# First attention layer: the last 64 rows of two projections share the array, and every engine's order of work is written anew

## The chip, the cores and the metric

The kernel runs on one core of one Trainium2 chip. The metric is the time of one execution on the device in microseconds (us), as the median of several. Abbreviations: PE is the matmul engine TensorE, DVE is VectorE, ACT is ScalarE, POOL is GpSimd, SP is SyncE, which here only starts DMAs. DMAs move data between the device memory and the on-chip memory SBUF; matmuls write to the accumulator memory PSUM, which has banks.

## The reference, cut to what matters

The program is a model of two layers on 64 sequences of 128 tokens with 256 features. Each layer is a cross attention followed by a feed forward part. Only the first attention and the routing of the first feed forward part are touched here:

```python
q = (x @ Wq).reshape(B, N, HEADS, hd)           # x: 256 features, normalized, 16 heads of 16
k = (context @ Wk).reshape(B, M, HEADS, hd)     # context: 192 features
v = (context @ Wv).reshape(B, M, HEADS, hd)
scores = einsum('bhid,bhjd->bhij', q, k) * scale    # then the mask
attn = softmax(scores)
out = einsum('bhij,bhjd->bhid', attn, v)
x = x + out @ Wo
...
logits = layernorm(x) @ w_switch + b_switch     # 8 experts
probs = softmax(logits);  routes = probs.argmax(-1)
pos = (cumsum(one_hot(routes), axis=0) * one_hot(routes)).sum(-1) - 1
keep = pos < capacity                           # row goes to slot routes*capacity+pos
```

The context has 192 features, so a contraction over it is one full step of 128 rows and one half step of 64 rows.

## The kernel before, in words

The function phase_first_layer takes two sequences at a time, a "job"; there are 32 jobs, numbered 0 to 31. A job consists of pieces with short names, and four tables of text say in which order each engine takes them. A table entry such as `K:2` in a cyclic table (FIRST_PE_ORDER and its siblings) means that in turn k of the cycle piece K of job k-2 is done. A HEAD table gives the first pieces by job number, a TAIL table the last ones, counted back from the end (`O:1` is job 31); `headed` and `ended` put them around the cycle. The order is fixed when the program is built; on the chip each engine works through its list, and waits at semaphores for its inputs.

The pieces on PE:

- Tx transposes the normalized rows, Q, K and V are the projections (four matmuls each, 128x256 per matmul; a trace counts each float32 matmul twice, so it shows x8).
- S0 and S1 are the two rounds of scores of a job. One round fills all four PSUM banks of scores: four matmuls bring the mask in (L702), then 16 matmuls with 32 rows each (L711). Bank r may only be refilled when ACT has made the exponentials of the round before from it.
- T0.0, T0.1, T1.0, T1.1 transpose the normalized probabilities (L721), A multiplies them with the values (L732, outputs of 32 partitions each), O is the output projection.
- Tn transposes the normalized new rows, L multiplies them with the routing weights (output of 8 columns), r.n counts tokens per expert.
- F0 to F5 and B0 to B5 multiply weights for a later phase; they only need loaded weights.

Products other than scores go to four PSUM banks in turn. A piece waits until what lay in its bank four products earlier has been copied out.

On DVE, `S0.x2` is the row maximum of bank 2 of round S0, `S0.i2` the reciprocal of its row sums, a name with ^ (`K^`, `A^`, `Tn^`) copies that product out of PSUM, st and st1 are statistics of rows, mk makes mask rows. The routing has three pieces there: r.sh, r.oh and r.n^. They exist once per group of jobs, for jobs 3, 7, 11, 15, 19, 23, 27, 29 and 31. I call a turn of the cycle in which they occur a routed turn, the others plain ones. r.oh is a chain of about sixteen small dependent operations (L617 to L626), r.n^ one of six (L632 to L639). On ACT, `S0.e2` are the four exponentials of bank 2, `T0^2` a copy of a transposed bank, nm the normalization of rows. On POOL, `S0.n2` divides a bank's probabilities by their sums, rs, rs1 and nm1 normalize, put sends rows to their experts' slots (two indirect DMAs).

On SP, load(j) fetches the rows x and the context of job j. The context has two buffers; a load of job j waits until K and V of job j-2 are done. The rows have four buffers, and load(j) waits for nm1 of job j-4. The layout in memory (function lay_out, unchanged) repeats the last 64 context rows in both halves of a second 128-row block, and fills the missing 64 rows of the key weights with zeros below, those of the value weights with zeros above. K and V thus each do a second full 128-row step in which half of the rows are zeros.

The second layer, which the change does not touch, already has the paired form for its own f.K and f.V (L1653, L1662, L1664, L1665).

Of the kernel before, what the change touches and what calls it, by code (L numbers as in the profile page):

```python
# [146 lines left out]
S1.x3:0 S1.x0:0 S1.x2:0 Tx^:2 S1.i1:0 V^:0 K^:1 st:3 mk:4 K^:2 S0.x2:1 S1.i0:0 S0.x3:1 S0.x1:1 S0.i1:0 S0.x0:1
V^:1 S1.i3:0 S1.x3:1 S1.x2:1 S1.x1:1 S0.i1:1 S1.x0:1 S1.i2:0 Q^:2 S0.i0:1 S1.i0:1 S0.x0:2 S1.i1:1 S1.i2:1
S0.x2:2 S0.i3:1 S0.i2:1 A^:0 S0.x3:2 S0.x1:2 V^:2 S1.i3:1 O^:0 st1:0 S0.i3:2 S0.i1:2 S1.x2:2 S1.x3:2 S1.x1:2
Tx^:3 S1.x0:2 K^:3 Q^:3 st:4 S0.x1:3 S0.x2:3 S1.i2:2 S0.x0:3 S0.i0:2 S1.i1:2 S1.i3:2 S1.i0:2 A^:1 S0.x3:3  # L150
S0.i1:3 S0.i2:2 S0.i0:3 V^:3 O^:1 st1:1 S1.x0:3 S1.x1:3 Tx^:4 S1.x3:3 K^:4 S1.x2:3 Q^:4 S0.i3:3 st:5 S1.i1:3
# [1646 lines left out]
```

## Time and profile before

| | us |
|---|---|
| median of 3 runs (4029.2 to 4032.24) | 4030.45 |
| the profiled execution's own time | 4034.15 |
| its span, first to last instruction | 4032.1 |
| start to score round S1 of job 5 | 106.05 |
| from there to S1 of job 28 (23 turns) | 408.48 |
| from there to S1 of job 31 (mask at 568.00) | 53.47 |
| from there to the first matmul of the experts' phase (629.24) | 61.24 |
| busy over the whole span: PE / ACT / DVE / POOL | 3956.1 / 2656.5 / 2384.4 / 1852.6 |

Only the first 629 us belong to the changed phase. In a timeline, a row gives the start, the duration, engine, line, operation, output<-inputs, shapes and how many instructions were merged; in square brackets stands how long the engine was idle before it and whom it waited for. A matmul's recorded duration is longer than its share of PE, since matmuls overlap; the time that a piece takes is therefore read as the difference of two starts. A windows row gives, for each engine, the busy time and the number of instructions in that stretch, then the granted PE clock (1.00 is the full 2.4 GHz), the DMA share and GB/s. The granted clock is 1.00 in all of the middle part.

### The profile page before, as it was taken

The page shows a single profiled execution, that of the slowest core. Times are in us where ns is not written, and L with a number is a line of the kernel's source. Part 1 is how long each engine was busy: PE and PEld are TensorE (multiplying, and loading weights), DVE is VectorE, ACT ScalarE, POOL GpSimd, SP SyncE. Part 2 cuts the span into 40 slices and gives each one's busy share as a digit, 9 for nine tenths or more (in the row PEclk, how much of TensorE's full clock was granted, in tenths as well). Part 3 has the DMA queues.
Part 4 walks back from the last instruction along what each step waited for, and adds up shares of the span by engine and source line. Part 5 has one row for each costly group of instructions (what it writes and reads, how often), then busy time and mean ns, then how long its engine had stood idle before and what let it go on. Part 6 is the DMA issues. An engine that isn't in the chain of part 4 may idle for free.

```text
span 4032.1 us, 100880 instructions
## 1 busy us (share of the span) xinstructions
PE 3956.1 (98%) x38276; PEld 3369.6 (84%) x38276; DVE 2384.4 (59%) x6216; ACT 2656.5 (66%) x11851; POOL 1852.6 (46%) x1979
## 2 busy tenths in 40 slices
PE   8999999999999999999999999999999999999998
PEld 6888876667888888888888888888888888888887
DVE  6888871125566566566656656666556656666554
ACT  8998971124666666666666666666666666666765
POOL 5787872113434444444444444444444444444434
PEclk9999998999999999999999999999999999999999
DMA  3232214520000000000000000000000000000000
GB/s 103 74 106 76 67 58 147 166 81 25 15 12 15 17 14 14 14 14 14 14 13 13 14 13 21 12 12 12 13 12 12 12 12 12 13 13 12 4 4 9
DMA packets 117868, 129.74 MB, mean 32 GB/s; under 512 B 12007, under 2 KB 110677, under 8 KB 117265
## 3 DMA queue, kind: packets, MB, share of 16 engines
q1 hardware_dynamic: 105648, 109.80, 8.5%
q0 software_dynamic: 6144, 8.43, 0.7%
q8 instruction: 311, 5.10, 0.5%
q10 hardware_dynamic: 5600, 5.07, 0.4%
q14 instruction: 165, 1.34, 0.1%
HBM read 89.68 MB, written 41.94 MB: 33 GB/s over the span
## 4 chain that ended last, share of the span: by engine, by line
PE 76%; DVE 1%; ACT 1%; POOL 0%; issue 0%; DMA 0%; POOLq 0%; DVEq 0%
PE c_product L1552 35%; PE c_product L1563 14%; PE c_product L1614 11%; PE c_scores L1604 7%; PE c_product L1637 5%; PE c_product L1625 2%; PE c_product L1653 1%; PE c_product L1664 1%; DVE c_qT L1407 1%; PE c_product L1540 1%; PE c_product L1662 1%; ACT c_front_probs L1364 0%; ACT c_probs L1364 0%; PE c_product L1691 0%; DVE c_neg_max L1416 0%
## 5 line engine op out<-in xcount | busy, mean ns | idle before, releaser
L1318 POOL TENSOR_TENSOR c_probs<-c_probs,c_row_inv 128x512 f32<-128x512 f32 x744 | 766.5, 1042 | 1436.6 <-DVE c_row_inv L1419 1432.9
L1364 ACT ACTIVATE c_probs<-c_scores,c_neg_max 128x128 f32<-128x128 f32 x2976 | 1054.9, 398 | 432.7 <-DVE c_neg_max L1416 432.4
L1552 PE MATMUL c_product<-c_nodes,cell_w 128*128 128x256 f32 x4352 | 1049.7, 382 | 1.5 <-DVE c_nodes L1478 0.8
L1552 PEld LDWEIGHTS c_product<-c_nodes,cell_w 128*128 128x128 f32 x4352 | 794.8, 190 | 108.8 <-issue 7.3
L1416 DVE TENSOR_REDUCE c_neg_max<-c_scores 128x4 f32<-128x512 f32 x1024 | 664.7, 676 | 104.9 <-PE c_scores L1604 98.9
L1364 ACT ACTIVATION_READ_ACCUMULATOR c_probs<-c_scores,c_neg_max 128x1 f32 x2976 | 703.5, 236 | 0.0
L1370 ACT COPY c_probsT<-c_product 128x512 f32<-128x512 f32 x744 | 416.6, 616 | 235.9 <-PE c_product L1614 229.4
L1364 ACT ACTIVATE c_front_probs<-c_scores,c_neg_max 128x128 f32<-128x128 f32 x1120 | 404.6, 406 | 176.6 <-DVE c_neg_max L1416 176.4
L1563 PE MATMUL c_product<-cell_w,c_nodes 128*128 128x256 f32 x1792 | 435.3, 383 | 0.5 <-DVE c_x L1469 0.5
L474 ACT ACTIVATE a_probs<-a_scores,a_neg_max 128x128 f32<-128x128 f32 x1024 | 360.4, 410 | 47.9 <-DVE a_neg_max L545 47.6
L1614 PE MATMUL c_product<-consts_sb,c_probs 128*128 128x128 f32 x2976 | 385.8, 273 | 0.1
L1318 POOL TENSOR_TENSOR c_front_probs<-c_front_probs,c_row_inv 128x512 f32<-128x512 f32 x280 | 287.1, 1041 | 202.7 <-DVE c_row_inv L1419 202.0
L1614 PEld LDWEIGHTS c_product<-consts_sb,c_probs 128*128 128x128 f32 x2976 | 347.4, 141 | 37.6 <-POOL c_probs L1318 0.9
L1563 PEld LDWEIGHTS c_product<-cell_w,c_nodes 128*128 128x128 f32 x1792 | 330.3, 190 | 56.5 <-issue 15.4
L1407 DVE TENSOR_SCALAR c_qT<-c_product,cell_b 128x256 f32<-128x256 f32 x372 | 162.7, 478 | 288.7 <-PE c_product L1552 288.5
L1552 PE MATMUL c_product<-c_oT,cell_w 128*128 128x256 f32 x1240 | 318.4, 379 | 0.1
L427 POOL TENSOR_TENSOR a_probs<-a_probs,a_row_inv 128x512 f32<-128x512 f32 x256 | 264.9, 1056 | 80.7 <-DVE a_row_inv L548 80.6
L1419 DVE RECIPROCAL c_row_inv<-c_row_sum 128x4 f32<-128x4 f32 x1024 | 168.5, 169 | 222.6 <-ACT c_probs L1364 195.1
L1407 DVE TENSOR_SCALAR c_kT<-c_product,cell_b 128x256 f32<-128x256 f32 x372 | 162.7, 478 | 227.4 <-PE c_product L1552 227.3
L1364 ACT ACTIVATION_READ_ACCUMULATOR c_front_probs<-c_scores,c_neg_max 128x1 f32 x1120 | 273.2, 244 | 0.0
L1552 PEld LDWEIGHTS c_product<-c_oT,cell_w 128*128 128x128 f32 x1240 | 235.4, 190 | 32.8 <-DVE c_oT L1407 0.8
L474 ACT ACTIVATION_READ_ACCUMULATOR a_probs<-a_scores,a_neg_max 128x1 f32 x1024 | 252.9, 249 | 0.0
(185 smaller groups left out, 6457.8 us busy)
## 6 DMA issues: line engine op xcount, KB each, us to landing
e_w<-in_L_ffn_w SPq DMA_DIRECT2D x12, 1024.0 KB, 6.3
a_x<-in_x SPq DMA_DIRECT2D x32, 256.0 KB, 3.0
a_ctxT<-in_ctx_pairsT SPq DMA_DIRECT2D x32, 256.0 KB, 3.4
x<-a_x SPq DMA_DIRECT2D x32, 256.0 KB, 2.1
...
```

The source lines that it names most:

```text
L427: nc.gpsimd.tensor_tensor(p, p, rinv[:, j % 2, b, r].unsqueeze(2).broadcast_to([P, 4, T]), ALU.mult).then_inc(norm_made, 1)
L474: a = nc.scalar.activation(pr[:, j % 2, b, r, k], S[r][:, k], ACT.Exp, bias=nmax[:, j % 2, b, r, k:k + 1], accum_out=rsum[:, j % 2, b, r, ...
L1318: nc.gpsimd.tensor_tensor(e, e, rinv[:, i, r].unsqueeze(2).broadcast_to([P, 4, T]), ALU.mult).then_inc(norm_made, 1)
L1364: a = nc.scalar.activation(probs(n, j)[:, r, k], S[r][:, k], ACT.Exp, bias=nmax[:, i, r, k:k + 1], accum_out=rsum[:, i, r, k:k + 1])
L1370: nc.scalar.copy(probsT(n, j)[:, int(n[-1])], bank(n, j)[:]).then_inc(pT_made, 1)
L1407: k = V.tensor_scalar(dst[:, u], m[:, u], bias[:, u:u + 1], scalar, ALU.add, *([then] if then else []))
L1416: V.tensor_reduce(nmax[:, i, r], S[r][:], AX.X, ALU.max, negate=True).then_inc(max_made, 1)
L1552: i = T_.matmul(m[:, u], w[:, k, u * P:(u + 1) * P], src[:, k], start=n == 0, stop=n == last)
L1563: i = T_.matmul(m[:, b], src[:, k, b * T:(b + 1) * T], w[:, k], start=n == 0, stop=n == len(steps) - 1)
L1604: i = T_.matmul(S[r][:, k], q[e, u, b * T:(b + 1) * T], w[e, u, b * T:(b + 1) * T], start=True, stop=True)
L1614: i = T_.transpose(m[:, k], probs(name, j)[:, r, k], ident)
L1637: i = T_.matmul(m[32 * r:32 * r + 32, u, b * T:(b + 1) * T], vs[g][:, b, h:h + 32], pTs[g][:, r, k], start=True, stop=True)
```

## The change

It has two parts. First, where K of job j is directly followed by V of job j-1 in the PE order, the two are done together: each does its full 128-row step, and then the two half steps of 64 rows run as pairs, the keys' half on rows 0 to 63 of the array and the values' half on rows 64 to 127, with different outputs. The semaphore for both products comes after the last pair. Elsewhere K and V are done as before. The new order has 26 such pairs (K of jobs 3 and 5 to 29); the old order has no place where V of job j-1 follows K of job j.

```diff
+            for (n, j), after in zip(on_pe, on_pe[1:] + [None]):
...
                 elif n == "K":
...
+                    if after != ("V", j - 1):
+                        project(product(n, j), wk, ct[:, o]).then_inc(prod, 1)
+                    else:
+                        keys_m = product(n, j)
+                        for u in range(2):
+                            T_.matmul(keys_m[:, u], wk[:, 0, u * P:(u + 1) * P], ct[:, o, 0], start=u == 0, stop=False)
                 elif n == "V":
...
+                        for b in range(PAIR):
+                            T_.matmul(m[:, b], ct[:, o, 0, b * T:(b + 1) * T], wv[:, 0], start=b == 0, stop=False)
+                        for u in range(2):
+                            k = T_.matmul(keys_m[:, u], wk[half[0], 1, u * P:(u + 1) * P], ct[half[0], 1 - o, 1], start=False, stop=u == 1)
+                            v = T_.matmul(m[:, u], ct[half[1], o, 1, u * T:(u + 1) * T], wv[half[1], 1], start=False, stop=u == 1)
+                        k.then_inc(prod, 1)
+                        v.then_inc(prod, 1)
```

Second, all tables of the four engines are replaced: cycle, head and tail, and ACT gets a tail of its own, which it did not have:

```diff
 FIRST_PE_ORDER = """
-Tn:6 Q:1 T0.1:3 T1.1:3 S0:1 A:3 r.n:7 K:0 O:3 T1.0:2 T0.0:2 S1:1 L:6 Tx:0 V:1
+K:2 V:3 Q:2 L:8 T0.1:4 T1.1:4 S0:2 A:4 Tn:7 Tx:1 r.n:8 O:4 T1.0:3 T0.0:3 S1:2
...
 FIRST_PE_HEAD = """
-K:0 Tx:0 Q:0 S0:0 Tx:1 V:0 K:1 Q:1 S1:0 Tx:2 K:2 S0:1 V:1 T0.0:0 T1.0:0 S1:1 Q:2 T0.1:0 T1.1:0 S0:2 A:0 V:2
+K:0 Tx:0 Q:0 S0:0 K:1 Tx:1 V:0 Q:1 S1:0 K:2 Tx:2 V:1 S0:1 T0.0:0 T0.1:0 S1:1 Q:2 Tx:3 T1.0:0 T1.1:0 S0:2 A:0
...
-    on_pe, on_dve, on_pool = (ended(tail, order, JOBS) for tail, order in (
+    on_pe, on_dve, on_act, on_pool = (ended(tail, order, JOBS) for tail, order in (
```

PE in a plain turn of the middle, before, from one L to the next round's transposes of probabilities and scores:

```order
L688 MATMUL a_product<-a_wsw,a_xn1T 128x8 x4
L674 MATMUL a_product<-consts_sb,a_xn 128x128 x4
L688 MATMUL a_product<-a_wv,a_ctxT 128x256 x4
L674 MATMUL a_product<-consts_sb,a_xn 128x128 x4
L681 MATMUL a_product<-a_xT,a_wq 128x256 x4
L721 MATMUL a_product<-consts_sb,a_probs 128x128 x16
L702 MATMUL a_scores<-a_mask_add,a_one_row 128x512 x4
```

and now, from the end of round S1 to the next round S0:

```order
L731 MATMUL a_scores<-a_kT_odd,a_qT 128x128 x4
L773 MATMUL a_product<-a_ctxT,a_wk 128x256 x2
L783 MATMUL a_product<-a_wv,a_ctxT 128x256 x2
L785 MATMUL a_product<-a_ctxT,a_wk 128x256
L786 MATMUL a_product<-a_wv,a_ctxT 128x256
L785 MATMUL a_product<-a_ctxT,a_wk 128x256
L786 MATMUL a_product<-a_wv,a_ctxT 128x256
L698 MATMUL a_product<-a_xT,a_wq 128x256 x4
L705 MATMUL a_product<-a_wsw,a_xn1T 128x8 x4
L741 MATMUL a_product<-consts_sb,a_probs 128x128 x16
L722 MATMUL a_scores<-a_mask_add,a_one_row 128x512 x4
```

V has moved from the stretch after S1 into the pair with K, and K has moved out of the stretch between S0 and S1, where it used to stand behind A; into that stretch go Tn and Tx. The cycle between two rounds S0 and S1 now holds A, Tn, Tx, O and two T, that between S1 and the next S0 the pair, Q, L and two T.

DVE in a routed turn, before, from the first three maxima of round S0 (L545) to the copies of the keys (L562, L563); the six rows L632 to L639 are r.n^:

```order
L545 TENSOR_REDUCE a_neg_max<-a_scores 128x4 x3
L570 COPY a_oT<-a_product 128x512
L632 TENSOR_TENSOR a_place<-a_product,a_one_hot 128x64
L635 TENSOR_REDUCE a_pos<-a_place 128x8
L636 TENSOR_SCALAR a_kept<-a_pos 128x8
L637 TENSOR_SCALAR a_route<-a_route 128x8
L638 TENSOR_TENSOR a_pos<-a_pos,a_route 128x8
L639 TENSOR_TENSOR slots<-a_pos,a_kept 128x8
L548 RECIPROCAL a_row_inv<-a_row_sum 128x4
L545 TENSOR_REDUCE a_neg_max<-a_scores 128x4
L562 TENSOR_SCALAR front_keys<-a_product,consts_sb 128x512
L563 TENSOR_SCALAR a_kT_odd<-a_product,consts_sb 128x512
```

and now (the same operations have lines 17 higher):

```order
L562 TENSOR_REDUCE a_neg_max<-a_scores 128x4 x3
L565 RECIPROCAL a_row_inv<-a_row_sum 128x4
L587 COPY a_oT<-a_product 128x512
L596 COPY a_xn1T<-a_product 128x512
L649 TENSOR_TENSOR a_place<-a_product,a_one_hot 128x64
L652 TENSOR_REDUCE a_pos<-a_place 128x8
L653 TENSOR_SCALAR a_kept<-a_pos 128x8
L654 TENSOR_SCALAR a_route<-a_route 128x8
L655 TENSOR_TENSOR a_pos<-a_pos,a_route 128x8
L656 TENSOR_TENSOR slots<-a_pos,a_kept 128x8
L574 COPY a_xT<-a_product 128x512
L562 TENSOR_REDUCE a_neg_max<-a_scores 128x4
```

Two more copies, of Tn and of Tx, stand between the third and the fourth maximum; the copies of the keys have moved behind the next round's maxima. In both orders r.oh stands before the first maximum of S0; the row statistics st, which came between r.oh and that maximum, now come ahead of r.oh.

PE at the end of the phase, before, from O of job 31 (a_wo) on:

```order
L688 MATMUL a_product<-a_wo,a_oT 128x256 x4
L688 MATMUL a_product<-a_wsw,a_xn1T 128x8 x4
L674 MATMUL a_product<-consts_sb,a_xn 128x128 x4
L688 MATMUL a_product<-a_wsw,a_xn1T 128x8 x4
L674 MATMUL a_product<-consts_sb,a_xn 128x128 x4
L688 MATMUL a_product<-a_wsw,a_xn1T 128x8 x4
L674 MATMUL a_product<-consts_sb,a_xn 128x128 x4
L767 MATMUL a_product<-a_one_hot,consts_sb 128x32
L768 MATMUL a_product<-a_tokens_before,consts_sb 128x32
L688 MATMUL a_product<-a_wsw,a_xn1T 128x8 x4
L681 MATMUL a_product<-a_edge_w,a_edgeT 128x256 x4
L782 MATMUL a_product<-be,a_edge_w 128x1 x4
```

and now:

```order
L705 MATMUL a_product<-a_wo,a_oT 128x256 x4
L691 MATMUL a_product<-consts_sb,a_xn 128x128 x4
L698 MATMUL a_product<-a_edge_w,a_edgeT 128x256 x4
L705 MATMUL a_product<-a_wsw,a_xn1T 128x8 x4
L804 MATMUL a_product<-a_one_hot,consts_sb 128x32
L805 MATMUL a_product<-a_tokens_before,consts_sb 128x32
L691 MATMUL a_product<-consts_sb,a_xn 128x128 x4
L705 MATMUL a_product<-a_wsw,a_xn1T 128x8 x4
L698 MATMUL a_product<-a_edge_w,a_edgeT 128x256 x4
L819 MATMUL a_product<-be,a_edge_w 128x1 x4
L804 MATMUL a_product<-a_one_hot,consts_sb 128x32
L805 MATMUL a_product<-a_tokens_before,consts_sb 128x32
```

Fewer L and Tn are left behind O of job 31, F2 (the a_edge_w row) now stands between Tn and L of job 30, and F3 directly behind L of job 31.

## Rows read from the trace of the kernel before

**Rows 1.** Windows: middle part, one plain turn, end of the phase.

```profile
106.05:514.53 408.48, 394.79 (x4989) 348.03 (x4989) 334.50 (x932) 372.88 (x1706) 329.79 (x384) 1.00 0.25 81
320.94:337.77 16.83, 16.83 (x220) 15.04 (x216) 13.81 (x36) 15.83 (x75) 15.25 (x18) 1.00 0.24 77
602.00:617.00 15.00, 14.21 (x54) 12.47 (x54) 7.90 (x38) 0.29 (x2) 10.89 (x11) 0.54 0.09 23
```

**Rows 2.** Timeline of PE, a routed and a plain turn.

```profile
307.45 0.40 PE L702 MATMUL a_scores<-a_mask_add,a_one_row 32*128 32x512 bf16 x4
...
319.72 0.39 PE L702 MATMUL a_scores<-a_mask_add,a_one_row 32*128 32x512 bf16 x4
...
322.32 1.89 PE L688 MATMUL a_product<-a_wv,a_ctxT 128*128 128x256 f32 x8
324.05 0.60 PE L674 MATMUL a_product<-consts_sb,a_xn 128*128 128x128 f32 x4
324.49 1.89 PE L681 MATMUL a_product<-a_xT,a_wq 128*128 128x256 f32 x8
...
328.06 0.39 PE L702 MATMUL a_scores<-a_mask_add,a_one_row 32*128 32x512 bf16 x4
...
331.16 1.99 PE L681 MATMUL a_product<-a_ctxT,a_wk 128*128 128x256 f32 x8
332.99 1.89 PE L688 MATMUL a_product<-a_wo,a_oT 128*128 128x256 f32 x8
...
336.56 0.40 PE L702 MATMUL a_scores<-a_mask_add,a_one_row 32*128 32x512 bf16 x4
```

**Rows 3.** Timeline of PE, a pair f.K and f.V of the second layer.

```profile
1292.00 1.13 PE L1653 MATMUL c_product<-c_ctxT,c_wk 128*128 128x256 f32 x4
...
1294.99 1.13 PE L1563 MATMUL c_product<-cell_w,c_nodes 128*128 128x256 f32 x4
1295.96 1.03 PE L1563 MATMUL c_product<-cell_w,c_oT 128*128 128x256 f32 x4
```

**Rows 4.** Timeline of PE, the waits of the routed turn.

```profile
314.31 1.99 PE L688 MATMUL a_product<-a_wo,a_oT 128*128 128x256 f32 x8 [1.18 <-DVE a_oT L570]
...
318.56 1.22 PE L721 MATMUL a_product<-consts_sb,a_probs 128*128 128x128 f32 x8 [1.39 <-DVE a_kT_odd L563]
```

**Rows 5.** Timeline of DVE, the routed turn.

```profile
306.42 0.21 DVE L617 TENSOR_REDUCE a_mx<-a_exp 128x8 f32<-128x64 f32 x1
...
311.79 1.87 DVE L545 TENSOR_REDUCE a_neg_max<-a_scores 128x4 f32<-128x512 f32 x3
...
314.18 0.21 DVE L632 TENSOR_TENSOR a_place<-a_product,a_one_hot 128x64 f32<-128x64 f32 x1
...
316.44 0.66 DVE L545 TENSOR_REDUCE a_neg_max<-a_scores 128x4 f32<-128x512 f32 x1
```

**Rows 6.** Timelines of ACT (first exponential of two rounds) and PE between.

```profile
91.69 0.37 ACT L474 ACTIVATE a_probs<-a_scores,a_neg_max 128x128 f32<-128x128 f32 x1 [0.24 <-DVE a_neg_max L545]
...
97.53 0.40 PE L702 MATMUL a_scores<-a_mask_add,a_one_row 32*128 32x512 bf16 x4 [0.29 <-ACT a_probs L474]
...
99.64 0.37 ACT L474 ACTIVATE a_probs<-a_scores,a_neg_max 128x128 f32<-128x128 f32 x1 [0.32 <-DVE a_neg_max L545]
```

**Rows 7.** Timeline of DVE, the longest wait for rows of x.

```profile
346.63 0.75 DVE L512 BATCH_NORM_STATS2 a_stats<-a_x 128x6 f32<-128x256 f32 x2 [2.00 <-DMA a_x<-in_x]
```

**Rows 8.** Timeline of ACT in the head, before the third round's exponentials.

```profile
34.15 0.37 ACT L474 ACTIVATE a_probs<-a_scores,a_neg_max 128x128 f32<-128x128 f32 x1 [4.28 <-DVE a_neg_max L545]
```

**Rows 9.** Timelines of the end: PE, DVE, PE.

```profile
514.53 0.66 PE L702 MATMUL a_scores<-a_mask_add,a_one_row 32*128 32x512 bf16 x4
...
597.16 0.95 PE L688 MATMUL a_product<-a_wsw,a_xn1T 128*128 128x8 f32 x8
...
617.49 0.19 DVE L632 TENSOR_TENSOR a_place<-a_product,a_one_hot 128x32 f32<-128x32 f32 x1 [2.63 <-PE a_product L681]
...
629.24 1.94 PE L888 MATMUL e_turned<-consts_sb,front_keys 128*128 128x128 f32 x8 [6.10 <-PEq L259]
```

More of the change, by code:

```diff
@@ L128 @@
+K^:3 V^:4 Q^:3 L^:9 r.sh:9 S1.i0:4 st:2 S0.i1:4 S1.i3:4 mk:2 r.oh:9 S0.i0:4 S0.i2:4 S0.x2:3 S0.x1:3
 """
 FIRST_ACT_ORDER = """
-nm:-1 T0^1:1 S1.e3:0 S1.e2:0 S1.e1:0 r.ex:5 S1.e0:0 T0^3:1 T0^2:1 T1^3:1 T1^2:1 S0.e2:-1 S0.e3:-1 S0.e0:-1
-S0.e1:-1 T1^0:0 T1^1:0 T0^0:0
+S0.e0:4 T1^0:5 T1^1:5 T0^0:5 T0^1:5 S1.e1:4 S1.e0:4 S1.e2:4 S1.e3:4 T0^3:5 r.ex:9 T0^2:5 T1^2:5 T1^3:5 nm:2
+S0.e2:3 S0.e1:3 S0.e3:3
 """
 FIRST_POOL_ORDER = """
-S0.n3:2 nm1:4 put:11 S0.n1:2 S1.n0:2 rs:0 S0.n2:2 S1.n1:2 S0.n0:2 S1.n2:2 S1.n3:2 rs1:3
+S0.n2:3 S0.n0:3 S1.n2:3 S0.n3:3 rs1:4 nm1:4 put:11 S1.n0:2 rs:0 S1.n1:2 S1.n3:2 S0.n1:2
@@ L147 @@
[L147 to L151, printed above, removed]
@@ L157 @@
[L157 to L160 removed]
+nm:0 nm:1 S0.e0:0 S0.e1:0 S0.e3:0 S0.e2:0 nm:2 S1.e3:0 S1.e2:0 S1.e1:0 S1.e0:0 nm:3 S0.e1:1 S0.e0:1 S0.e3:1
@@ L178 @@
 """
 FIRST_POOL_TAIL = """
-put:8 rs1:1 nm1:1 put:7 put:6 put:5 put:4 put:3 put:2 put:1
+S0.n1:3 nm1:5 S1.n0:3 S0.n2:3 S1.n1:3 put:12 put:11 S0.n0:3 rs:1 S1.n3:3 S0.n3:3 S1.n2:3 put:10 rs1:4 S0.n3:2
+nm1:4 S0.n0:2 S0.n1:2 S0.n2:2 put:9 S1.n0:2 S0.n3:1 rs1:3 S1.n1:2 S1.n2:2 S1.n3:2 S0.n1:1 nm1:3 S0.n0:1
+S1.n2:1 S1.n0:1 S0.n2:1 S1.n1:1 S1.n3:1 put:8 put:7 rs1:2 nm1:2 put:6 rs1:1 nm1:1 put:5 put:4 put:3 put:2
+put:1
+"""
+FIRST_ACT_TAIL = """
+T0^2:4 T0^3:4 T1^2:4 T1^3:4 S0.e0:2 S0.e3:2 S0.e2:2 T1^1:3 T1^0:3 S0.e1:2 T0^0:3 nm:1 T0^1:3 S1.e1:2 S1.e0:2
@@ L689, in project_rows @@
                 return i
-            for n, j in on_pe:
+            keys_m = None
+            half = slice(0, P // 2), slice(P // 2, P)
+            for (n, j), after in zip(on_pe, on_pe[1:] + [None]):
                 o = j % 2
@@ L751, in _ @@
                     pe.wait_ge(wv_in, 16)
-                    project_rows(product(n, j), wv, ct[:, o]).then_inc(prod, 1)
+                    m = product(n, j)
+                    if keys_m is None:
+                        project_rows(m, wv, ct[:, o]).then_inc(prod, 1)
+                    else:
+                        for b in range(PAIR):
[5 more added lines that the diff above has]
+                        v.then_inc(prod, 1)
+                        keys_m = None
                 elif n == "O":
```

52 lines of the change are left out of this document (32 added, 20 removed).

## The prediction, made before the changed kernel was run

> **What bounds the kernel now.** I read the page's busy shares first: PE is busy 98% of the whole span, so PE time is what counts, unless some other engine holds it up. Only the first 629 us are touched, so I asked for windows over that phase. In the middle part, 23 turns from round S1 of job 5 to round S1 of job 28, PE is busy 394.79 of 408.48 us, and ACT 372.88 [rows 1]. In a plain turn PE never rests, ACT is busy 15.83 of 16.83, POOL 15.25, DVE 13.81. The reader should see that PE is the bound there and that ACT and POOL are close behind: whatever PE saves beyond about one microsecond per turn, it cannot have. Then the timeline of PE: a plain turn, from one S1 mask to the next, takes 336.56 - 319.72 = 16.84, of which 8.34 lie between S1 and S0 and 8.50 between S0 and S1 [rows 2]. A routed turn is 3.77 longer, all of it between S0 and S1 (319.72 - 307.45 = 12.27 against 8.50). PE waits there for two copies by DVE, 1.18 and 1.39 [rows 4], and DVE is late because r.oh (from 306.42) pushes the maxima of S0 to 311.79, and r.n^ (from 314.18) pushes the fourth maximum to 316.44 [rows 5]. At the end of the phase the granted clock is 0.54, mostly the lower level of 1.2 GHz [rows 1]. The chain of waits says the same at large: most of it is PE. The program's time is thus the phase's length plus a part that does not change.
>
> **The pair.** V and K take 324.05 - 322.32 = 1.73 and 332.99 - 331.16 = 1.83 on PE [rows 2], 3.56 together. The second layer shows the new form with the same shapes: 1294.99 - 1292.00 = 2.99 [rows 3]. The matmul piece after it starts slower, 0.97 for four records where V needs 1.73 for eight, so 0.10 more; I take this as the cost of going from parts of the array back to the whole. Today K pays such 0.10 behind A (1.83 against 1.73) and L behind S1. In the new order Tn pays behind A, the pair's 2.99 already holds it behind S1, Q pays behind the pair, and L, behind Q, no longer does. PE work of a plain turn: 16.84 - 3.56 + 2.99 + 0.10 + 0.10 - 0.10 = 16.37. So the pair saves 0.47 a turn on PE, 26 pairs about 12 us, were nothing else in the way. Bounds: from nothing (the pair as slow as two whole pieces) to 0.86, half of a piece, if changing the form were free.
>
> The trace thus charges about 0.3 us for entering and leaving the halved array. The Trainium skill, page "TensorEngine Tiling (Array Packing)", section "Key Properties", speaks against the change: changing the tiling mode drains TensorE. It gives no price; by that rule alone a pair could eat its own gain, and the sum would be the 0 of the bounds above. The 2.99 us of the trace contain both changes of mode, so the measurement decides, and the trace agrees that they are not free.
>
> **What takes its place in a plain turn.** Each round of scores uses all four banks, so there is a loop that PE's work doesn't shorten: exponentials of one round, then the next mask, scores, maxima, exponentials. Where it was bare in the old trace it took 97.53 - 91.69 = 5.84 from the first exponential to the mask, and 99.64 - 97.53 = 2.11 from there to the next exponential [rows 6], 7.95 in all. Today the two distances are 8.34 and 8.50, both longer. In the new order the stretch from S0 to S1 loses K (1.83) and gets Tn and Tx (0.44 each, by 324.49 - 324.05) and 0.10: 8.50 - 1.83 + 0.88 + 0.10 = 7.65. That is less than 7.95, so PE will wait 0.30 for ACT at the mask of S1. The last exponentials of S0 in ACT's order are those of bank 0, and the masks start with bank 0, so all four wait. The other stretch has 16.37 - 7.65 = 8.72 and is PE's. A plain turn: 8.72 + 7.95 = 16.67, a gain of 0.17, and 23 of them 3.9 us.
>
> **A routed turn.** There are five in the stretch (groups 3, 7, 11, 15, 19), before and after. The order of r.oh before S0's maxima is kept. I count DVE from the S1 mask: Q is finished after a round (1.2), the pair and Q, 6.0; its copy, the logits, r.sh, the statistics and three reciprocals follow (0.2 + 0.6 + 0.1 + 0.4 + 1.2 + 0.3), so r.oh begins near 8.9 to 9.1, 0.2 to 0.4 behind S0's mask at 8.72. Before, it began 1.03 ahead of it (306.42 against 307.45). r.oh takes about 4.1 (306.42 to 311.79 less 1.3 for statistics and reciprocals), so the first maximum starts 4.3 to 4.7 behind the mask, and it was 4.34 [rows 2, 5]. Then come three maxima (1.8), A^ and Tn^ (0.6 each), r.n^, Tx^ (0.6) and the fourth maximum. r.n^ takes 2.1 in the middle part [rows 5], when POOL is at work; if POOL rests, perhaps half. The fourth maximum starts 9.1 to 10.6 behind the mask; with 0.7 for it, 1.4 for four exponentials and 0.35 to the mask of S1 the stretch is 11.6 to 13.1, against 7.95 in a plain turn: 3.6 to 5.1. I take 4.4, near the middle, since POOL will partly rest. Against 3.77 today this loses 0.6 five times, 3.2 us. PE's own wait for A^ and for two freed banks lies within it. The middle part as a whole: 3.9 - 3.2, a gain of 0.7.
>
> On r.n^ the two readings differ for a reason that the Trainium skill gives, page "SBUF — State Buffer", section "SBUF: two separate sides": DVE operations with two SBUF inputs and POOL's exclude each other on a shared port pair. By that rule a routed turn would lose the 3.6 if POOL has run out of reciprocals by then, and the 5.1 if it has not; no row here shows which it will be.
>
> **Head.** ACT stood idle for 4.28 before the third round [rows 8]: V^:0 stands late in DVE's old list, K:2 waited for its bank, and the clock fell. The new head has V^:0 and K:2 earlier. But st:3 now stands ahead of S1's maxima and waits for rows of x that are loaded only after V:0, and from the second round on ACT's own work sets the pace. I take 2 of the 4.28; ends -1 (slower) and 4.
>
> **Last rounds.** From S1 of job 28 to the end of O of job 31 the old trace has 597.16 - 514.53 = 82.6 [rows 9]. Laying the new PE list out with the times above (a round 1.21, a T half 0.92, L 0.82, A 1.9, a projection 1.73, F as one, B 0.88) gives 8.7 + 10.8 (routed, without r.n^ in the way) + 8.3 + 12.0 + 7.95 + 8.0 + 23.3 = 79.1, with the same F0, F1, B0, B1 inside. Such a sum sees only waits that I looked for, so I count 2 of the 3.5; ends 0 and 5.
>
> **Drain.** From there to the experts' first matmul it is 629.24 - 597.16 = 32.1. The last routing count was stuck behind F2 and B2 at the lower clock, and DVE got it only at 617.49 [rows 9], though its inputs were ready some 6 us earlier. Now F2 fills a wait before it, and F3 and B2 fit while DVE computes r.oh. POOL also has fewer put left over. I take 5; ends 0 (the clock falls as before and the next F sits on it) and 7.
>
> **Sum** on the profiled execution: 4034.15 - 2 - 0.7 - 2 - 5 = 4024.5. The median lies 3.7 below that execution (4030.45 against 4034.15), so 4020.7, and I say 4020.5.
>
> **Rivals.**
> (B) The orders fit better than I see: the loop is hidden because masks of the first banks go ahead, plain turns take 16.37 (23 x 0.47 = 10.8), routed turns lose 2 instead of 4.4 (5 x 1.8 = 9 against today), head 4, last rounds and drain 9 together: 33 less, about 3998. For it: PE's work really shrinks. Against it: r.oh still stands before S0's maxima.
> (C) The loop and r.oh take all and the drain keeps its low clock: middle part 3 slower (routed 5.1 each, so 6.6 lost against 3.9), head 1, last rounds 2, drain 2 gained: 2 less, 4028.5. For it: the low clock comes from thin work after O of job 31, and that is as thin as before.
> (D) Slower. The wait for the rows of x becomes one of every turn. DVE has waited up to 2.00 for them [rows 7]. Their load starts behind nm1 of four jobs earlier, and POOL has 15.25 us of work in a turn of 16.67; when nm1 ends 2 us later than I lay it out, st ends after S0's scores, and each microsecond beyond that lengthens the turn, since maxima and exponentials stand in the loop. At one microsecond of lateness a plain turn takes 17.5: 23 x 0.66 = 15 lost, and with the other terms 7 slower, 4039. I lay st out at 7.3 behind the S1 mask; with its 1.2 and the reciprocals' 0.3 it must start by 8.6 for the maxima to start on time, 1.4 behind S0's mask at 8.72. So this decides from 1.3 us of lateness on, 0.7 less in turns with mk. Against it: today st has no such room at all.
> (E) The change doesn't do what it says: if the two halves ran one behind the other, K and V would take 3.56 or more and turns stay at 16.84; then 4024 to 4027, inside C. The second layer's rows speak against it [rows 3].
>
> **How the numbers follow.** Forecast 0.42, B 0.18, C and E 0.26, D 0.14. A measurement of this kernel can tell about 0.2%, 8 us, from no change: faster means below 4022.4, slower above 4038.5. The forecast's own spread, some 6 us either way, lies to 0.29 below that bound and 0.13 within; B is faster; C is within except 0.06; D is slower to 0.10. Faster 0.29 + 0.18 + 0.06 = 0.53, same 0.13 + 0.20 + 0.04 = 0.37, slower 0.10. The range 4003 to 4034 leaves out the better part of B and D; the forecast's own is 4014 to 4027.
>
> **What would show it.** Pair: from the first K matmul to the next piece 2.99. Loop: waits of PE at the S1 mask for ACT, 0.3 each, and plain turns of 16.6 to 16.7; none of them and 16.4 would be B. Routed turns 20.3 to 21.8 long, with DVE's fourth maximum late. Drain: r.n^ of job 31 within 15 us of the end of O instead of 20. If DVE waits for x by more than half a microsecond in plain turns, it is D. If head and drain are unchanged, my sum is short by 7 and C holds.

## The result, and the profile after

The changed kernel took 4057.73 us (median of 4 runs, 4055.56 to 4059.33); the kernel before took 4030.67 in the same comparison (4 runs, 4029.2 to 4032.24). The ratio is 1.0069, with a 95% interval of 1.0057 to 1.0082: 27 us slower, where 10 us faster was forecast. Three executions in a slow state (5077 us of the kernel before, 5394 of warm and 6442 of split_end, all below) are left out of every median that follows.

The time was lost in three stretches of the first phase. The traces give them so; the last column is what the prediction laid out:

| stretch | before | after | change | forecast |
|---|---|---|---|---|
| start to S1 of job 5 | 106.05 | 109.83 | +3.8 | -2 |
| to S1 of job 28, 23 turns | 408.48 | 425.52 | +17.0 | -0.7 |
| to the end of O of job 31 | 82.63 | 93.36 | +10.7 | -2 |
| to the experts' first matmul | 32.08 | 27.99 | -4.1 | -5 |

The windows show the same stretches: the middle part, in it six microseconds of a routed turn and one plain stretch, then the last rounds and the drain (total time, busy time and instructions of PE, PE weight load, DVE, ACT, POOL, then the granted clock, DMA share, GB/s).

```profile
109.83:535.35 425.52, 396.67 (x4989) 340.19 (x4990) 333.74 (x931) 378.41 (x1708) 329.65 (x384) 0.96 0.24 78
328.11:334.48 6.37, 6.37 (x24) 5.38 (x25) 4.37 (x15) 5.31 (x25) 1.95 (x4) 0.56 0.12 41
343.20:351.20 8.00, 7.74 (x133) 6.89 (x133) 6.18 (x15) 8.00 (x38) 7.84 (x10) 1.00 0.04 15
535.35:628.71 93.36, 84.04 (x965) 73.99 (x965) 61.93 (x181) 62.96 (x271) 68.03 (x75) 0.93 0.14 45
628.71:656.70 27.99, 20.76 (x97) 18.17 (x96) 14.12 (x57) 0.23 (x1) 13.22 (x14) 0.72 0.28 88
```

PE was busy 396.67 in the middle part, more than the 394.79 of [rows 1], although its work had shrunk; the granted clock of the whole part is 0.96 instead of 1.00. So first: where does PE run slower? The timeline of PE in the routed turn of job 17 answers, from the mask of S0 to the mask of S1:

```profile
319.44 0.40 PE L722 MATMUL a_scores<-a_mask_add,a_one_row 32*128 32x512 bf16 x4
...
322.54 1.09 PE L691 MATMUL a_product<-consts_sb,a_xn 128*128 128x128 f32 x8
325.52 0.41 PE L804 MATMUL a_product<-a_one_hot,consts_sb 128*128 128x64 f32 x2 [1.89 <-DVE a_tokens_before L643]
...
328.11 3.75 PE L705 MATMUL a_product<-a_wo,a_oT 128*128 128x256 f32 x8 [1.96 <-DVE a_oT L587]
331.65 2.90 PE L741 MATMUL a_product<-consts_sb,a_probs 128*128 128x128 f32 x16
334.48 0.39 PE L722 MATMUL a_scores<-a_mask_add,a_one_row 32*128 32x512 bf16 x4
```

This answers to [rows 2, 4]. The stretch takes 15.04 where it took 12.27. PE waits 1.89 and 1.96, and then O takes 331.65 - 328.11 = 3.54 and the two T 2.83 instead of 1.8 and 1.9. DVE in the same stretch, which answers to [rows 5]: the first and the last operation of r.oh, its additions, the first maxima, the first and the last operation of r.n^, the fourth maximum.

```profile
319.80 0.18 DVE L634 TENSOR_REDUCE a_mx<-a_exp 128x8 f32<-128x64 f32 x1
...
321.54 0.69 DVE L641 TENSOR_TENSOR a_one_hot<-a_iota_less_E,a_route 128x64 f32<-128x64 f32 x1
322.27 3.11 DVE L643 TENSOR_TENSOR a_tokens_before<-a_tokens_before,a_one_hot 128x8 f32<-128x8 f32 x8
...
325.45 1.85 DVE L562 TENSOR_REDUCE a_neg_max<-a_scores 128x4 f32<-128x512 f32 x3
...
328.48 0.21 DVE L649 TENSOR_TENSOR a_place<-a_product,a_one_hot 128x64 f32<-128x64 f32 x1
...
329.46 0.17 DVE L656 TENSOR_TENSOR slots<-a_pos,a_kept 128x8 uint32<-128x8 f32 x1
...
330.14 0.68 DVE L562 TENSOR_REDUCE a_neg_max<-a_scores 128x4 f32<-128x512 f32 x1
```

The eight additions took 3.11, two of them 0.91 and 0.97 and the others 0.17 each. POOL's timeline shows what stood beside them, three multiplications by reciprocals of 1.04 each:

```profile
321.04 3.11 POOL L444 TENSOR_TENSOR a_probs<-a_probs,a_row_inv 128x512 f32<-128x512 f32 x3
```

In the old trace the additions took 1.57, and POOL, which had ended a multiplication at 307.6, rested until 310.81:

```profile
309.01 1.57 DVE L626 TENSOR_TENSOR a_tokens_before<-a_tokens_before,a_one_hot 128x8 f32<-128x8 f32 x8
...
310.81 1.04 POOL L427 TENSOR_TENSOR a_probs<-a_probs,a_row_inv 128x512 f32<-128x512 f32 x1 [3.21 <-DVE a_row_inv L548]
```

Plain turns came out nearly as forecast. PE at four masks, S0, S1, S0, S1:

```profile
343.20 0.40 PE L722 MATMUL a_scores<-a_mask_add,a_one_row 32*128 32x512 bf16 x4
...
351.20 0.40 PE L722 MATMUL a_scores<-a_mask_add,a_one_row 32*128 32x512 bf16 x4 [0.26 <-ACT a_probs L491]
...
360.01 0.40 PE L722 MATMUL a_scores<-a_mask_add,a_one_row 32*128 32x512 bf16 x4
...
368.50 0.40 PE L722 MATMUL a_scores<-a_mask_add,a_one_row 32*128 32x512 bf16 x4 [0.72 <-ACT a_probs L491]
```

S0 to S1 takes 8.00 with a wait for ACT (forecast 7.95 and 0.30), and 8.49 where mk stands in the turn; S1 to S0 takes 8.81 here (8.72 to 8.74, the forecast, in 14 of the 23 turns).

### The profile page after: what moved, and what is told of

It is laid out like the page before. It is cut to its first block, busy times and chain, and to the rows that moved or that the text cites. A ratio compares the mean times of both kernels' runs of the same rounds, so it can differ in the third digit from the quotient of the medians.

```text
span 4057.5 us, 100881 instructions
## 1 busy us (share of the span) xinstructions
PE 3963.8 (98%) x38276; PEld 3367.1 (83%) x38276; DVE 2388.3 (59%) x6216; ACT 2662.2 (66%) x11851; POOL 1853.5 (46%) x1979
## 4 chain that ended last, share of the span: by engine, by line
PE 76%; DVE 1%; ACT 0%; POOL 0%; issue 0%; DMA 0%; POOLq 0%; DVEq 0%
PE c_product L1589 35%; PE c_product L1600 14%; PE c_product L1651 10%; PE c_scores L1641 7%; PE c_product L1674 5%; PE c_product L1662 2%; PE c_product L1690 1%; PE c_product L1701 1%; DVE c_qT L1444 1%; PE c_product L1577 1%; PE c_product L1699 1%; ACT c_front_probs L1401 0%; PE c_product L1728 0%; ACT c_probs L1401 0%; DVE c_neg_max L1453 0%
## 5 line engine op out<-in xcount | busy, mean ns | idle before, releaser
L1453 DVE TENSOR_REDUCE c_neg_max<-c_scores 128x4 f32<-128x512 f32 x1024 | 664.9, 676 | 102.3 <-PE c_scores L1641 96.3
L491 ACT ACTIVATION_READ_ACCUMULATOR a_probs<-a_scores,a_neg_max 128x1 f32 x1024 | 244.6, 239 | 0.0
```

The costliest lines, as they stand in the source:

```text
L491: a = nc.scalar.activation(pr[:, j % 2, b, r, k], S[r][:, k], ACT.Exp, bias=nmax[:, j % 2, b, r, k:k + 1], accum_out=rsum[:, j % 2, b, r, ...
L1453: V.tensor_reduce(nmax[:, i, r], S[r][:], AX.X, ALU.max, negate=True).then_inc(max_made, 1)
```

## The experiments

Theory 1: the loss sits in the routed turns. The routing's work on DVE stands ahead of maxima for which the loop of scores, maxima and exponentials waits; POOL makes it slower (1b), and PE's two waits bring the clock down (1c). Rival: the paired form costs more than it seemed. Theory 2: the new end tables cost time. Theory 3: a plain turn is PE's work in one stretch and ACT's loop in the other. Each run was compared with the kernel before on the same chip; differences are given against it, since its median moved between 4028.9 and 4029.9. The changed kernel is 27.1 slower in that count. Where two changed kernels are compared with each other, they mostly ran on different chips, so differences of 2 to 4 us between them are near the noise.

**no_pair.** The condition for pairing is never true:

```diff
-                    if after != ("V", j - 1):
+                    if True:
```

> The changed kernel with all its new tables, but K and V done whole, one behind the other (eight matmuls each, nothing left out of the result). Theory 1 (the loss of 27 us sits in the routed turns, the pair itself pays): K and V take 3.56 where the pair takes 2.99 and Q loses its slow start, so the stretch from S1 to S0 grows from 8.72 to about 9.2; with 26 pairs some 12 us more, 4070. Rival (the pair's form costs more than the trace of the second layer showed, and is the loss): no slower than the changed kernel, 4057 or less.

Measured: 4062.55, ratio 1.0081 (1.0067 to 1.0094), 33.6 slower than before, 6.5 slower than with pairs. PE at the mask of S1, behind S1, and the next mask:

```profile
335.73 0.40 PE L722 MATMUL a_scores<-a_mask_add,a_one_row 32*128 32x512 bf16 x4
...
336.95 1.99 PE L698 MATMUL a_product<-a_ctxT,a_wk 128*128 128x256 f32 x8
338.78 1.89 PE L705 MATMUL a_product<-a_wv,a_ctxT 128*128 128x256 f32 x8
340.51 1.89 PE L698 MATMUL a_product<-a_xT,a_wq 128*128 128x256 f32 x8
...
344.92 0.39 PE L722 MATMUL a_scores<-a_mask_add,a_one_row 32*128 32x512 bf16 x4
```

K and V take 3.56, the stretch 344.92 - 335.73 = 9.19 against 8.72: the 0.47 of the sum, exactly. The pair pays, and the rival falls. But only half of 26 x 0.47 arrives. In the profiled executions the other stretches are longer with pairs: the five routed ones take 74.0 together against 71.7 here, and S0 to S1 of job 6 takes 9.74 against 7.99, for a wait of 1.67 for rows of x that is absent here.

**quiet.** Three reciprocals of DVE, on which POOL's multiplications wait, go behind r.oh:

```diff
-... S1.x2:4 S1.i1:4 K^:3 ... S1.i0:4 st:2 S0.i1:4 S1.i3:4 mk:2 r.oh:9 S0.i0:4
+... S1.x2:4 K^:3 ... S1.i0:4 st:2 mk:2 r.oh:9 S1.i1:4 S0.i1:4 S1.i3:4 S0.i0:4
```

> The changed kernel with S1.i1, S0.i1 and S1.i3 of DVE moved behind r.oh, so that POOL has no reciprocals to work with while DVE does r.oh. Theory 1b (r.oh takes 5.5 instead of 4.1 because its small operations with two inputs wait for whole operations of POOL): the eight additions at the end of r.oh take 1.6 instead of 3.11, r.oh ends about 2 us earlier, but r.n^ then falls beside POOL and takes 2.1 instead of 1.06; routed turns 1 to 3 us shorter, six of them, 4040 to 4052. Rival (r.oh is slow for a reason of its own, such as its wait for DVE's own queue): the additions stay at 3.1 and the time at 4057.

Measured: 4044.14, ratio 1.0034 (1.002 to 1.0047), 12 better than the changed kernel. DVE's additions and the end of r.n^, and PE at O and at S1, which stands 12.95 behind S0's mask (313.01):

```profile
315.29 1.57 DVE L643 TENSOR_TENSOR a_tokens_before<-a_tokens_before,a_one_hot 128x8 f32<-128x8 f32 x8
...
321.19 0.89 DVE L655 TENSOR_TENSOR a_pos<-a_pos,a_route 128x8 f32<-128x8 f32 x1
322.11 0.97 DVE L656 TENSOR_TENSOR slots<-a_pos,a_kept 128x8 uint32<-128x8 f32 x1
```

```profile
319.78 3.11 PE L705 MATMUL a_product<-a_wo,a_oT 128*128 128x256 f32 x8 [2.15 <-DVE a_oT L587]
...
325.96 0.40 PE L722 MATMUL a_scores<-a_mask_add,a_one_row 32*128 32x512 bf16 x4 [0.31 <-ACT a_probs L491]
```

Theory 1b is shown: with POOL idle the same additions take 1.57, and r.n^, now beside POOL, takes 2.9 (320.15 to 323.00) where it took 1.06. PE still runs at a granted clock of 0.72 in the six microseconds from O on.

**warm.** Work added to keep PE busy; its results are not used:

```diff
+                    warm(16 if j < 24 else 0)
                     pe.wait_ge(hot, g + 1)
+                    warm(12 if j < 24 else 0)
```

> The changed kernel; PE does 28 more transposes of constants into the bank of r.n, 16 before it waits for the one-hot rows and 12 behind that wait, in the routed turns of jobs 3 to 23. Their results are overwritten by r.n. Theory 1c (PE waits twice in a routed turn, its granted clock falls to the lower level, and the O and the T behind it take 3.5 and 2.8 instead of 1.8 and 1.9): with PE kept at work the clock stays at 1.00, O takes 1.8, S1 starts 2.0 earlier; five turns, 10 us less, 4047 to 4049. Rival (ACT and DVE set the end of the stretch, PE's slowness is hidden): no change, or 1 to 3 slower for the added work.

Measured: 4052.79 (five runs, 4045.4 to 4053.5), ratio 1.0054 (1.0041 to 1.0067): 3 better than the changed kernel by the medians, where 9 to 11 were expected. In the trace, of a run of 4045.39, PE from the added transposes (merged under L805) to the mask of S1, and the window of O and T:

```profile
317.01 3.50 PE L805 MATMUL a_product<-consts_sb 128*128 128x128 f32 x28
...
321.65 1.97 PE L705 MATMUL a_product<-a_wo,a_oT 128*128 128x256 f32 x8 [0.75 <-DVE a_oT L587]
323.45 2.29 PE L741 MATMUL a_product<-consts_sb,a_probs 128*128 128x128 f32 x16
326.05 0.40 PE L722 MATMUL a_scores<-a_mask_add,a_one_row 32*128 32x512 bf16 x4 [0.31 <-ACT a_probs L491]
```

```profile
321.50:326.00 4.50, 3.96 (x24) 3.21 (x24) 4.18 (x15) 4.07 (x24) 1.31 (x2) 1.00 0.01 3
```

The stretch takes 326.05 - 312.98 = 13.07, 1.97 less than 15.04, and PE again waits for ACT. O starts 8.67 behind the mask of S0 in both kernels, so nothing before it differs. So 1c is shown for the stretch in this execution: 2 us of it were the clock. The five routed stretches of the middle part fell from 74.0 to 65.4 together. In the last rounds the transposes lengthened two stretches by 2.3, and the one behind them was 2.1 shorter. Why three runs took 7 us more than the profiled one is open, and with it whether those runs kept the clock up as this one did.

**late.** r.oh goes behind st1, r.n behind Q, r.n^ behind Q^:

```diff
-... A^:6 Tn^:9 r.n^:10 Tx^:3 S0.x0:4 O^:6 S0.i3:5 st1:6 S1.x1:4 ... mk:2 r.oh:9 S0.i0:4
+... A^:6 Tn^:9 Tx^:3 S0.x0:4 O^:6 S0.i3:5 st1:6 r.oh:10 S1.x1:4 ... Q^:3 r.n^:10 L^:9 ... mk:2 S0.i0:4
```

> The changed kernel with r.oh moved from before the maxima of S0 to behind st1, into DVE's idle 1.8 before the maxima of S1, r.n of PE moved behind Q of the next stretch and r.n^ behind Q^. Theory 1 (the maxima of S0 behind r.oh are what costs 6 to 7 us in each routed turn, since they stand in the loop of scores, maxima and exponentials and DVE has no idle time there): the stretch from S0 to S1 of a routed turn falls from 14 to 15.3 to about 8.5, that from S1 to S0 grows by 1.7 to 3, six turns, 18 to 28 less: 4030 to 4040. Rival (r.oh costs the same wherever it stands, DVE being the bound): within 5 us of 4057.

Measured: 4040.9, ratio 1.0029 (1.0018 to 1.004), 15 better, 0.9 above the range expected. The routed stretch is 8.51, but the two behind it are 10.39 and 11.04. POOL's timeline tells why:

```profile
333.07 1.10 POOL L469 DMA_INDIRECT buf<-a_xn,slots  x1 [6.15 <-DVE slots L656]
```

POOL stands 6.15 before a put, and the divisions of the probabilities are queued behind it. The edit brought this wait in by placing r.n^ so late: in split, where r.n^ comes earlier, it is 1.95.

**split.** r.oh is cut: the additions become r.tb, behind st1; r.n follows S1 at once.

```diff
+                    elif n == "r.tb":
                         for t in range(w):
-... st1:6 S1.x1:4 S1.x3:4 S1.x0:4 S1.x2:4 S1.i1:4 K^:3
+... st1:6 r.tb:10 S1.x1:4 S1.x3:4 S1.x0:4 S1.x2:4 S1.i1:4 r.n^:10 K^:3
```

> The changed kernel with r.oh cut in two: its first eight operations stay where they are, its eight additions (now r.tb) stand behind st1, in DVE's idle 1.8 before the maxima of S1; r.n of PE stands right behind S1 and r.n^ before K^, so that the slots are ready when POOL comes to its puts (with the whole r.oh moved there POOL waited 6.15 for them). Theory 1 (what a routed turn costs is the routing's DVE time in front of maxima that the loop waits for, plus what follows from it: POOL's operations beside it and PE's clock): the stretch from S0 to S1 falls from 14 to 15.3 to 9.0 to 9.5, the next ones stay at 8.7 to 9.2 and 8.5; six turns with 5 less each, 4024 to 4030. Rival (the moved whole r.oh cost 4.9 a turn because DVE has no room, not because of POOL's wait): 4038 or more.

Measured: 4033.69 (11 runs), ratio 1.001 (1.0001 to 1.0019): 23 of the 27 us are back. That is 3.7 above the expected 4024 to 4030 and below the rival's 4038. PE's masks S0, S1, S0 of a routed turn and O between them:

```profile
309.65 0.40 PE L723 MATMUL a_scores<-a_mask_add,a_one_row 32*128 32x512 bf16 x4
...
315.21 1.99 PE L706 MATMUL a_product<-a_wo,a_oT 128*128 128x256 f32 x8 [1.37 <-DVE a_oT L587]
...
319.18 0.40 PE L723 MATMUL a_scores<-a_mask_add,a_one_row 32*128 32x512 bf16 x4 [0.23 <-ACT a_probs L491]
...
329.14 0.39 PE L723 MATMUL a_scores<-a_mask_add,a_one_row 32*128 32x512 bf16 x4
```

9.53 and 9.96; PE waits 1.37, and O runs at full clock. The middle part is 406.39, 2.1 less than in the old kernel. The next stretch was expected at 9.2 at most; it is longer because PE waits 0.73 for r.tb and the copy of K stands behind r.n^.

**cycle_end.** The changed kernel, with end tables built like the old ones behind the natural end of the new cycle:

```diff
-O:5 L:8 T1.0:4 T0.0:4 S1:3 Q:2 K:2 Tn:7 V:3 r.n:9 T0.1:4 S0:2 ...
+V:1 F0:1 L:6 T0.1:2 T1.1:2 B0:1 A:2 Tn:5 O:2 T1.0:1 T0.0:1 L:5 Tn:4 ...
```

> The changed kernel with the new cycle kept to its natural end, and behind it end tables built like those of the kernel before (V of job 31, F0, L of job 26 and so on behind the last S1; ACT without a table of its own). Theory 2 (the new end tables put more PE work between S0 and S1 of jobs 29 and 30 than ACT's loop leaves room for, and give it back in the drain): from S1 of job 28 to S1 of job 31 64.0 falls to 56.7, the rest to the experts' first matmul grows from 57.3 to 61 to 64; in all 4 less to nothing, 4053 to 4058. Rival (the new end tables lose time of their own): 4045 to 4050.

Measured: 4048.97, ratio 1.0048 (1.0034 to 1.0062), 8 better than the changed kernel. Windows from S1 of job 28 to the end of O of job 31, and from there to the experts:

```profile
531.61:617.31 85.70, 79.12 (x944) 68.95 (x945) 58.65 (x176) 62.38 (x270) 62.16 (x70) 0.94 0.18 58
617.31:646.64 29.33, 21.85 (x118) 19.51 (x116) 15.20 (x62) 0.46 (x2) 18.49 (x20) 0.78 0.19 58
```

115.0 against 121.35 in the changed kernel and 114.7 before. The new end tables lost 6.3; this kernel also pairs K and V of two more jobs, at most 0.9 of it. The rival was right: from S1 of job 28 to S1 of job 31 the time fell from 64.0 to 57.4, and the rest only grew from 57.3 to 57.6. Counted from the end of O of job 31, the new tables gain 1.3 in the drain.

**split_end.** Both tables together.

> Both together: the cut r.oh and the natural end of the cycle with end tables like those before. Theory 1 and 2: the gain of the cut, 28 to 34, and 0 to 4 of the end: 4020 to 4030, about the time of the kernel before or a little under it. Rival (DVE has no room): 4035 or more.

Measured: 4027.36 (10 runs), ratio 0.9994 (0.9985 to 1.0003). The two gains of 22.9 and 7.6 nearly add up (29.2), and it is no different from the old kernel's time.

**before_split.** The old kernel, no pairs, with the same cut:

```diff
-O^:3 S1.i3:2 st1:3 S0.i1:1 ... S1.x1:1 Tx^:0 ... A^:2 r.n^:6 S1.i2:1
+O^:3 S1.i3:2 st1:3 r.tb:7 S0.i1:1 ... S1.x1:1 r.n^:7 Tx^:0 ... A^:2 S1.i2:1
```

> The kernel before, without pairs, in its old order but for the routing: r.oh cut in two, its eight additions behind st1, r.n behind S1, r.n^ behind the maxima of S1. Theory 1: a routed turn's 3.77 beyond a plain one falls to 1.5 to 2; six turns, 11 to 14 less: 4016 to 4020, and the pair was not what the kernel lacked. Rival (in the old order DVE has only 0.6 idle before the maxima of S1, so the additions cost there what they cost before): within 4 of 4030.

Measured: 4018.37 (10 runs), ratio 0.9973 (0.9963 to 0.9982), 11 faster than the kernel before and the fastest of all. PE's masks S0, S1, S0 of a routed turn:

```profile
303.21 0.39 PE L703 MATMUL a_scores<-a_mask_add,a_one_row 32*128 32x512 bf16 x4
...
312.26 0.65 PE L703 MATMUL a_scores<-a_mask_add,a_one_row 32*128 32x512 bf16 x4
...
321.91 0.40 PE L703 MATMUL a_scores<-a_mask_add,a_one_row 32*128 32x512 bf16 x4
```

9.05 and 9.65 against 12.27 and 8.34: the routed turn is 1.9 shorter, by six turns the 11 us.

**balance.** As split_end, with L moved behind O:

```diff
-K:2 V:3 Q:2 L:8 T0.1:4 T1.1:4 S0:2 A:4 Tn:7 Tx:1 O:4 T1.0:3 T0.0:3 S1:2 r.n:8
+K:2 V:3 Q:2 T0.1:4 T1.1:4 S0:2 A:4 Tn:7 Tx:1 O:4 L:7 T1.0:3 T0.0:3 S1:2 r.n:8
```

> As the kernel with the cut r.oh and the end tables like those before (4027.8), but L of PE moved from the stretch between S1 and S0 (8.73, all PE work) into the stretch between S0 and S1, behind O, where PE has waited 0.26 in some turns and 0.72 in others for ACT's last exponentials; L^ stands behind O^. Theory 3 (a plain turn of the changed kernel is PE's work in one stretch, 8.73, plus ACT's loop in the other, 8.0 or 8.5 where mk makes it later): with L moved the stretches are 8.5 of PE work and 7.95, a plain turn 16.45 instead of 16.73 to 17.25; 23 turns, 8 to 11 less: 4017 to 4020. Rival (another loop, such as POOL's 15.25 of work or the rows of x, sets the turn's length): 4025 or more.

Measured: 4022.64 (11 runs), ratio 0.9984 (0.9975 to 0.9993): 5 better than split_end, 7 faster than before. PE's masks S0, S1, S0 in a plain turn:

```profile
327.65 0.39 PE L711 MATMUL a_scores<-a_mask_add,a_one_row 32*128 32x512 bf16 x4
...
336.19 0.40 PE L711 MATMUL a_scores<-a_mask_add,a_one_row 32*128 32x512 bf16 x4
...
344.08 0.39 PE L711 MATMUL a_scores<-a_mask_add,a_one_row 32*128 32x512 bf16 x4
```

8.54 and 7.89 without a wait, 16.43 in all: theory 3 holds for such a turn. In most of the turns with mk S0 to S1 is 9.0 to 9.3, and in several others 8.8. The median lies between the 4017 to 4020 of the theory and the 4025 of the rival; in the profiled executions the middle part takes 401.78 against 406.33 in split_end.

**balance_whole.** The same without pairs.

> The same kernel with K and V done whole instead of in pairs. Theory 3: where PE sets both stretches the pair's 0.47 is paid in full: 26 times 0.47, 12 more than with pairs, 4029 to 4032. Rival (the pair's gain stays hidden behind ACT's loop, as 5 of 12 us did in the changed kernel's order): 5 more or less.

Measured: 4031.53 (11 runs), ratio 1.0006 (0.9997 to 1.0015). The pair is worth 8.9 us here, of the 13.2 that its PE time promises for the 28 pairs of this order, and 6.5 of 12.2 in the changed kernel's own order. So theory 3's "paid in full" does not hold, and the gain is not hidden either.

**before_split2.** r.n behind L in the old order.

> The kernel before with the cut r.oh, and r.n of PE behind L instead of ahead of it, so that L fills PE's wait of 0.55 for r.tb. Theory 1: the wait goes, six routed turns 0.3 to 0.5 shorter, 4015 to 4018. Rival (r.n^ and with it S1's last maximum and the slots come later by what L takes, 0.8): 4018 to 4023.

Measured: 4020.81 (11 runs), ratio 0.9979 (0.997 to 0.9988), 2 slower than before_split by the medians, at the edge of the noise, and the middle part of the profiled execution is 2.0 longer (400.30 against 398.30): the rival. The wait for r.tb is gone, but S1 to the next S0 is 10.06 instead of 9.65, since r.n^ comes later and a Tn then waits 0.79 for a copy of logits.

**balance_mk.** mk moved behind st1:

```diff
-... st1:6 r.tb:10 S1.x1:4 ... S1.i3:4 mk:2 r.oh:9
+... st1:6 mk:3 r.tb:10 S1.x1:4 ... S1.i3:4 r.oh:9
```

> The kernel with the cut r.oh, L moved and the end tables like those before (4022.6), and mk of DVE moved from between st and the maxima of S0, where it stands beside POOL's rs, to behind st1, where DVE is idle for 1.8 to 2.5. Theory 4 (in every fourth turn mk and rs delay each other, so nm and the exponentials of S0 come later and the stretch from S0 to S1 takes 9.0 to 9.3 instead of 8.54): those turns fall to 8.6, five or six of them, 3 to 4 less, 4018 to 4020. Rival (these turns are late for the rows of x, which are loaded late there): 4021 to 4024.

Measured: 4026.47 (11 runs, 4020.6 to 4032.8), ratio 0.9991 (0.9982 to 1.0): 3.5 above balance against the kernel before, with intervals that overlap. DVE at mk, DVE at the next st, and POOL beside mk:

```profile
284.31 1.23 DVE L557 TENSOR_SCALAR a_mask_add<-a_mask_u 128x1024 bf16<-128x1024 uint8 x1
...
292.52 0.76 DVE L517 BATCH_NORM_STATS2 a_stats<-a_x 128x6 f32<-128x256 f32 x2 [0.58 <-DMA a_x<-in_x]
```

```profile
284.95 0.65 POOL L411 TENSOR_TENSOR a_var_eps<-a_mean_var,consts_sb 128x2 f32<-128x2 f32 x1
```

mk meets rs1 there instead of rs. S0 to S1 of the turns with mk did fall, from 9.0 to 9.3 down to 8.5 to 9.0, but the same stretch of the next turn is 8.8 to 9.4 where it was 8.5 to 8.8, so the middle part of the profiled execution is as long as before the move (401.56 against 401.78). The theory had the place right and gained nothing. That a later nm1, and with it a later load of rows, is what the next turn pays for fits the wait above, but no run tests it. The 4 us between the two profiled executions do not lie here at all: up to S1 of job 31 they differ by 0.5, and from there to the experts, with the same PE list, balance took 58.05 and balance_mk 61.76, at granted clocks of 0.87 and 0.77:

```profile
561.85:619.90 58.05, 45.77 (x406) 40.96 (x405) 29.86 (x114) 13.59 (x50) 37.91 (x39) 0.87 0.20 63
562.34:624.10 61.76, 53.48 (x405) 47.74 (x404) 30.28 (x114) 13.59 (x50) 37.88 (x39) 0.77 0.19 59
```

## Why the prediction was wrong

**The pair** was right: 2.99 on PE, 0.10 at the next piece, 0.47 a turn. The doubt that rested on the Trainium skill, page "TensorEngine Tiling (Array Packing)", section "Key Properties" (a change of tiling mode drains TensorE), is settled by no_pair: both changes are paid within those 2.99 and the 0.10 behind them.

**The plain turn** had the right mechanism: 8.72 and 7.95 forecast, 8.72 to 8.8 and 8.00 measured in a turn without mk. It left out mk: with it the stretch is 8.5, since mk's own 0.66 stands ahead of the maxima, and the first operation of rs takes 0.69 beside it instead of 0.20. It also left out waits for the rows of x, one of which made S0 to S1 of job 6 9.74. The 18 plain turns took 17.08 on average, against 16.98 before; forecast was a gain of 0.17 each. That is a loss of 1.8 us in place of a gain of 3.

**The routed turn** is the step that failed. It carries 15.3 of the 17 us: five turns of 22.7 to 24.1 where 20.3 to 21.8 was laid out (the turn with job 17: 15.04 from S0 to S1, where 11.6 to 13.1 was laid out). Three statements in it were wrong or short.
- "r.oh takes about 4.1" was read from the old trace, where POOL rested beside it. In the new order POOL works, and r.oh takes 5.5: the first maximum starts 6.0 behind the mask instead of 4.3 to 4.7. I had weighed this very effect for r.n^, with [rows 5], and did not ask it of r.oh in the line above. What I gave r.n^ for a resting POOL came true (1.06), and what it saved r.oh lost. The Trainium skill, page "SBUF — State Buffer", section "SBUF: two separate sides", says that a DVE operation with two SBUF inputs and a POOL operation that reads SBUF shut each other out for a whole instruction; the trace agrees, with additions of 0.91 and 0.97 beside multiplications of 1.04 where others take 0.17. The rule was at hand, and I used it for one of two pieces.
- The fourth maximum came 10.7 behind the mask, 0.1 beyond the range. By ACT alone S1 could have started 13.1 behind S0, the upper bound that was laid out.
- "PE's own wait for A^ and for two freed banks lies within it" was false, and this puts the stretch beyond its bounds. The first wait, 1.89, was for r.oh's additions and not in the list at all. Of the 4.5 us between Tx and O PE idles 3.9, its clock falls towards the lower level (0.56), and O and T become the last to finish, 2.0 later. warm shows the two parts apart.

**Head.** Forecast a gain of 2, measured a loss of 3.8 in the profiled run. Counted from the first mask, S1 of job 5 stood at 96.3 there and at 92.5 to 93.7 in the eight other traced kernels with this head and pairs; the old head had 91.3 to 92.6 in three. So the head itself costs about 1. Most of the rest is one stretch of that execution, S0 to S1 of job 2, 12.00 against 9.9 to 10.3 in the eight others: A took 3.50 there at a granted clock of 0.52, and 1.88 at 1.00 in late. A low clock just before it (0.72 from 31.4 to 47.1) is not what sets this execution apart, since it is 0.71 to 0.82 in the same stretch of the others. The wait before the third round [rows 8] had moved, not gone: ACT now idles 2.62, 2.27 and 1.07 before the exponentials of the second, third and fourth round. I had no sum for this part, only a share of one wait.

**Last rounds** were laid out as 8.7, 10.8, 8.3, 12.0, 7.95, 8.0 and 23.3; they took 8.7, 14.5, 9.8, 14.2, 8.7, 8.0 and 29.4. The first miss is the routed turn again (PE waited 4.39 there), and the 9.8 has a wait of 1.33 for a copy of K. The 14.2 runs at a granted clock of 0.88. In the last one PE waited 2.75 for r.oh's additions, and then ran at 0.60 for 7.3 us, in which an A took 3.6. The sum added work and left out what a wait does to the clock. cycle_end shows 6.3 of the loss to be the new end tables' own.

**Drain** was nearly right: 4.1 of 5, with r.n^ of job 31 at 16.2 behind the end of O where 15 was the sign and 20.3 the old value. The granted clock was no better (0.72 against 0.75), so the gain does not come from the clock.

Of the rivals, C had the mechanism nearest to what happened (r.oh takes all) with a price far too small. D's wait for rows of x was 8 us in six waits, against 13 in seventeen in the old kernel; it cost some 1.7 in job 6's turn and was not the main cause. D's sum is also off: 7 above the old median is 4037.5, not 4039. The failure of the range is that it bounded the routed turn by DVE and ACT alone. Two effects stood behind each other that it left out, a slower r.oh and PE's fallen clock.
